# Norms stored by one transfer, the Wo product in float32r pieces, and centring moved to ACT in the last stage

## What is computed

```python
xn = _layernorm(x)
# token diffusion on layer_norm(xn) * ln1_w + ln1_b, 16 heads of 16 columns
logits = (2 * qk @ qk.T - q2[:, None] - q2[None, :]) / sqrt(dh) * tau     # q2: squared norms of qk
y = xn + (softmax(logits) @ v) @ Wo_t * gamma1
# channel diffusion on layer_norm(y) * ln2_w + ln2_b, 8 heads of 32 channels
y = y + channel_diffusion(layer_norm(y)) * gamma2
# experts on xn: relu(xn @ W1[e] + b1[e]) @ W2[e] + b2[e], times the router's gate
out = x + y + moe(xn)
```

## Time and profile before

| | |
|---|---|
| median of 3 runs | 1292.47 us (1291.58 to 1297.14) |
| the profiled execution | 1292.76 us, span 1291.0 us |
| PE busy | 1251.0 us, 97% |
| ACT busy | 1041.8 us, 81% |
| DVE busy | 439.2 us, 34% |
| POOL busy | 211.6 us, 16% |
| mean granted clock of PE | 0.995 |

### The profile page before, as it was taken

How to read it: one execution, slowest core, us unless ns; L and a number is a source line. 1 busy time by engine, 2 the same in 40 slices (tenths; PEclk the granted TensorE clock), 3 DMA queues, 4 the chain that set the end, 5 groups by cost and what they waited for, 6 DMA issues and landing times. The chain is left out here.

```text
span 1291.0 us, 42753 instructions
## 1 busy us (share of the span) xinstructions
PE 1251.0 (97%) x18451; PEld 731.6 (57%) x18451; DVE 439.2 (34%) x1226; ACT 1041.8 (81%) x1181; POOL 211.6 (16%) x310
## 2 busy tenths in 40 slices
PE   7979999999999999999999999999999999999988
PEld 6744334555555555555555555555555555555877
DVE  6732001232222223223223223222222322225957
ACT  6869999888888888888888888888888888884120
POOL 3203441111100101111111111101011111102860
PEclk9989999999999999999999999999999999999999
DMA  6798347755564564654574556456456466533573
GB/s 191 248 283 189 94 94 229 151 135 138 153 148 118 160 141 112 175 143 122 137 184 122 132 122 186 125 159 145 109 151 157 121 150 171 162 120 121 135 139 123
DMA packets 161845, 193.48 MB, mean 150 GB/s; under 512 B 64280, under 2 KB 129304, under 8 KB 158200
## 3 DMA queue, kind: packets, MB, share of 16 engines
q1 hardware_dynamic: 148392, 168.84, 49.5%
q0 software_dynamic: 13264, 21.90, 7.0%
HBM read 154.63 MB, written 35.95 MB: 148 GB/s over the span
## 5 line engine op out<-in xcount | busy, mean ns | idle before, releaser
L994 ACT ACTIVATE shared<-ps 128x1024 f32<-128x1024 f32 x1024 | 969.1, 1040 | 122.5 <-PE ps L1135 122.1
L1158 PE MATMUL ps<-shared,work 128*17 128x256 f32 x7680 | 476.6, 380 | 0.0
L1135 PE MATMUL ps<-mov,stat 52*128 52x512 f32 x2048 | 346.2, 434 | 16.0 <-ACT shared L994 9.0
L1158 PEld LDWEIGHTS ps<-shared,work 128*17 128x17 f32 x7680 | 219.5, 98 | 149.8 <-issue 24.9
L1017 DVE TENSOR_TENSOR work<-ps,work 128x256 f32<-128x256 f32 x258 | 109.5, 424 | 565.1 <-PE ps L1180 562.8
L1135 PEld LDWEIGHTS ps<-mov,stat 52*128 52x128 f32 x2048 | 167.1, 185 | 202.7 <-issue 109.3
L1171 PE MATMUL ps<-XNW,work 128*32 128x256 f32 x2496 | 196.4, 390 | 0.2 <-issue 0.2
L1180 PE MATMUL ps<-work,XNW 128*32 128x128 f32 x4992 | 191.4, 273 | 0.3 <-issue 0.3
L1180 PEld LDWEIGHTS ps<-work,XNW 128*32 128x32 f32 x4992 | 148.8, 110 | 51.6 <-issue 0.8
L842 POOL DMA_DIRECT2D y_slots<-work x39 | 22.1, 567 | 553.2 <-DVE work L1023 505.6
L1171 PEld LDWEIGHTS ps<-XNW,work 128*32 128x32 f32 x2496 | 51.8, 108 | 107.0 <-issue 100.5
(11 more groups left out here) (177 smaller groups left out, 638.6 us busy)
## 6 DMA issues: line engine op xcount, KB each, us to landing
XNW<-in_L_ffn_W_dram SPq DMA_DIRECT2D x78, 1024.0 KB, 6.1
stat<-q_parts SPq DMA_DIRECT2D x192, 128.0 KB
mov<-q_parts SPq DMA_DIRECT2D x192, 64.0 KB
q_parts<-XNW SPq DMA_DIRECT2D x16, 512.0 KB, 5.1
x_slots<-work SPq DMA_DIRECT2D x1, 4992.0 KB, 17.6
early<-x_slots SPq DMA_DIRECT2D x156, 32.0 KB, 2.2
early<-in_L_ffn_b_dram SPq DMA_DIRECT2D x39, 128.0 KB, 8.0
y_slots<-work POOLq DMA_DIRECT2D x39, 128.0 KB, 2.0
```

The costliest lines, as they stand in the source:

```text
L994: nc.scalar.activation(probs[:, q % DEEP], ps[:, at:at + 2].rearrange("p a b -> p (a b)"), ACT.Exp, scale=head_scale).then_inc(probs_ready, 1)
L1135: last = nc.tensor.matmul(ps[:, at + r], stat[rows, head % 2, m * P:(m + 1) * P], mov[rows, head % 2, half * 512:(half + 1) * 512], start= ...
L1158: last = nc.tensor.matmul(ps[32 * j:32 * j + VW, AV, half * 256:(half + 1) * 256], Vh[:, head % 2, m], probs[:, q % DEEP, j * 256:(j + 1) ...
```

## The change

- **Norms.** `w_parts` takes the whole `wp` of a group, all 128 rows, in one transfer. `fill_stack` reads the two parts by transfers of their own: 20 for a head, not 16.
- **Start.** DVE takes the statistics of group 1 ahead of z of group 0, and scales the rest of the query weights apart from that of the value weights, which now stands behind the split of group 0; PE waits for it in the first `product_v`.
- **Heads' output.** `norm_o` turns o, copies it into an upper float32r part and subtracts for the rest. Both parts are stored: 8 transfers for a head. The last head's are issued by SP, ahead of the last part of XN, not by POOL.
- **Wo.** The scaled Wo is split once into two parts. `project` runs three float32r products in place of one in float32. `AT` has four slots of one group with two parts each; the groups of batch 1 are loaded as the projection of a group four earlier is done.
- **a2.** DVE stores the negated mean (`nmr`); POOL multiplies it by the root; ACT centres and scales (`make_z2`, four activations for each group, at hand-written places in its list); DVE multiplies by `l2w` and adds `l2b`, one operation each on 1024 columns.

```diff
-    w_parts = nc.dram_tensor("w_parts", [2, NB * H, S], F32).ap()
+    w_parts = nc.dram_tensor("w_parts", [GROUPS, P, 2, GN // 2], F32).ap()
...
         def store_w(G, par):
-            b, tok = G // GB, (G % GB) * GN
             nc.sync.wait_ge(w_split, G + 1)
-            for c in range(KC):
-                for k in range(2):
-                    at = 32 * (2 * c + k)
-                    nc.sync.dma_start(w_parts[:, bass.ds(b * H + c * HC, HC), bass.ds(tok + k * GN // 2, GN // 2)]
-                                      .rearrange("c h n -> h c n"), wp[at:at + HC, par]).then_inc(w_stored[par], 16)
+            nc.sync.dma_start(w_parts[G], wp[:, par]).then_inc(w_stored[par], 16)
...
             stats_x(0, 0)
+            stats_x(1, 1)
             make_z(0, 0)
-            rest_of_weights()
+            rest_of_query_weights()
             for k in range(KC):
                 rest_of_turned(0, 0, k)
-            stats_x(1, 1)
+            rest_of_value_weights()
...
-            at_least(nc.vector, o_stored, 16 * NCHUNK * head)
-            nc.vector.transpose(o_cols, o_rows).then_inc(o_ready, 1)
+            nc.vector.transpose(o_cols, o_rows).then_inc(o_flipped, 1)
+            nc.vector.wait_ge(o_flipped, head + 1)
+            at_least(nc.vector, o_stored, O_DMAS * 16 * head)
+            nc.vector.tensor_copy(o_parts[:, 0].bitcast(F32R), o_cols).then_inc(o_upper, 1)
+            nc.vector.wait_ge(o_upper, head + 1)
+            nc.vector.tensor_tensor(o_parts[:, 1].bitcast(F32R), o_cols, o_parts[:, 0], ALU.subtract).then_inc(o_ready, 1)
...
-                sp.wait_ge(v_copied, H)
-                sp.dma_start(AT[:, 0], a_turned[0:D].rearrange("(c p) n -> p c n", p=P)).then_inc(at_loaded[0], 16)
+                sp.wait_ge(v_copied, NB * H)
+                for G in range(GB):
+                    load_at(G)
...
+                store_o(sp, HEADS - 1, last_o_stored)
                 load_xn(2)
...
+                for G in range(GB, GROUPS):
+                    sp.wait_ge(wo_ready, 2 * (G - AT_SLOTS) + 2)
+                    load_at(G)
...
-                    nc.gpsimd.tensor_tensor(rs1[:, par], ve1[:, par], nhalf[:, 0], ALU.pow).then_inc(rstd3_ready, 1)
+                    nc.gpsimd.tensor_tensor(rs1[:, par], ve1[:, par], nhalf[:, 0], ALU.pow).then_inc(rs1_step, 1)
+                    pool.wait_ge(rs1_step, G + 1)
+                    nc.gpsimd.tensor_tensor(nmr[:, par], nmr[:, par], rs1[:, par], ALU.mult).then_inc(rstd3_ready, 1)
...
+                def make_z2(G, par):
+
+                    act.wait_ge(rstd3_ready, G + 1)
+                    at_least(act, gram_done, G - 1)
+                    if G >= 2:
+                        act.wait_ge(ring3_ready, use_a2(G - 2) + KC)
+                    for t in range(GT):
+                        last = nc.scalar.activation(a2g[:, par, t], XN[:, G * GT + t], ACT.Identity,
+                                                    bias=nmr[:, par, t:t + 1], scale=rs1[:, par, t:t + 1])
+                    last.then_inc(z2_ready, 1)
...
+                make_z2(0, 0)
+                make_z2(1, 1)
                 for G in range(GB):
                     take_a2(G, G % 2)
+                    if G + 1 < GB:
+                        make_z2(G + 2, G % 2)
 
                 take_gram(0)
+                make_z2(GB + 1, 1)
                 take_t(0)
                 for tt in range(3):
                     act.wait_ge(y_stored[tt], 16 * SLOT_USES)
                 take_a2(GROUPS - 4, 0)
+                make_z2(GROUPS - 2, 0)
                 take_a2(GROUPS - 3, 1)
                 exp_of(0)
+                make_z2(GROUPS - 1, 1)
                 take_a2(GROUPS - 2, 0)
                 take_r(0)
...
                 def make_a2(G, par):
...
+                    dve.wait_ge(z2_ready, G + 1)
+                    nc.vector.tensor_tensor(a2g[:, par], a2g[:, par], l2w[:, :].unsqueeze(1).broadcast_to([P, GT, D]),
+                                            ALU.mult).then_inc(a2_step, 1)
                     dve.wait_ge(a2_step, G + 1)
...
+                    nc.vector.tensor_tensor(a2g[:, par], a2g[:, par], l2b[:, :].unsqueeze(1).broadcast_to([P, GT, D]),
+                                            ALU.add).then_inc(a2_ready, 1)
...
+                            terms = [(a, w, c) for a, w in ((0, 0), (0, 1), (1, 0)) for c in range(KC)]
+                            for n, (a, w, c) in enumerate(terms):
+                                last = nc.tensor.matmul(ps[:, 2 + k, t * D:(t + 1) * D], AT[:, slot, a, c, cols],
+                                                        wo_parts[:, w, c], start=(n == 0), stop=(n == len(terms) - 1))
```

More of the change, by code:

```diff
@@ L300, in fill_stack @@
             r0 = i * 2 * DH + hh * DH
-            w = w_parts[:, bass.ds(i * 2 + hh, 1), :].rearrange("c h n -> (c h) n")
+            head = i * 2 + hh
+            row = 2 * 32 * (head % H // HC) + head % HC
+            w = w_parts[head // H * GB:(head // H + 1) * GB, row:row + 33:32].rearrange("g k c n -> c g k n")
             for r in range(2):
@@ L310, in fill_stack @@
                                  ).then_inc(stack_loaded[hh], 16)
-                sp.dma_start(stat_raw[at + AUX + 2:at + AUX + 4, hh], w).then_inc(stack_loaded[hh], 16)
-                sp.dma_start(mov_raw[at + AUX:at + AUX + 2, hh].rearrange("d (k n) -> d k n", k=2),
-                             w.rearrange("d (k r n) -> d r k n", r=2, k=2)[:, r]).then_inc(stack_loaded[hh], 16)
+                for part in range(2):
+                    sp.dma_start(stat_raw[at + AUX + 2 + part:at + AUX + 3 + part, hh].rearrange("d (g k n) -> d g k n", g=GB, k=2),
+                                 w[part].unsqueeze(0)).then_inc(stack_loaded[hh], 16)
+                    sp.dma_start(mov_raw[at + AUX + part:at + AUX + 1 + part, hh].rearrange("d (g k n) -> d g k n", g=2, k=2),
+                                 w[part, r::2].unsqueeze(0)).then_inc(stack_loaded[hh], 16)
         def x_rows(G):
@@ L708, in product_v @@
                     nc.tensor.matmul(bank, zT[:, par, 0, c, cols], wvr[:, c], start=(c == 0), stop=False)
+                if G == 0 and t == 0:
+                    pe.wait_ge(weights_scaled, 2)
                 for c in range(KC):
@@ L783, in build @@
         o_ready = sem("o_ready")
+        o_flipped = sem("o_flipped")
+        o_upper = sem("o_upper")
+        O_DMAS = 2 * NCHUNK
         o_stored = sem("o_stored")
+        last_o_stored = sem("last_o_stored")
         ex_ready = sem("ex_ready")
@@ L828, in build, with store_o, load_at @@
         xn_back = [sem(f"xn_back{k}") for k in range(3)]
-        at_loaded = [sem("at_loaded0"), sem("at_loaded1")]
+        at_loaded = [sem(f"at_loaded{k}") for k in range(AT_SLOTS)]
         HOMES = ((0, 1, 6, 7), (2, 3), (4, 5))
-        def store_o(head):
-            nc.gpsimd.wait_ge(o_ready, head + 1)
-            rows = a_turned[head * DH:(head + 1) * DH].rearrange("d (k j n) -> j d k n", k=2, j=NCHUNK)
+        def store_o(queue, head, stored):
+            queue.wait_ge(o_ready, head + 1)
             for j in range(NCHUNK):
-                nc.gpsimd.dma_start(rows[j], o_cols[32 * j:32 * j + DH].rearrange("d (k n) -> d k n", k=2)
-                                    ).then_inc(o_stored, 16)
+                for part in range(2):
+                    rows = a_turned[part, head * DH:(head + 1) * DH].rearrange("d (k j n) -> j d k n", k=2, j=NCHUNK)
+                    queue.dma_start(rows[j], o_parts[32 * j:32 * j + DH, part].rearrange("d (k n) -> d k n", k=2)
+                                        ).then_inc(stored, 16)
+        def load_at(G):
+            b, at = G // GB, (G % GB) * GN
+            for part in range(2):
+                nc.sync.dma_start(AT_raw[:, G % AT_SLOTS, part], a_turned[part, b * D:(b + 1) * D, at:at + GN]
+                                  .rearrange("(c p) n -> p c n", p=P)).then_inc(at_loaded[G % AT_SLOTS], 16)
         def store_y(n):
@@ L960, in _ @@
                         copy_v(head + 2)
-                        store_o(head)
+                        store_o(pool, head, o_stored)
                         head += 1
@@ L1283, in build @@
         a2_ready = sem("a2_ready")
+        z2_ready = sem("z2_ready")
+        rs1_step = sem("rs1_step")
         expert_added = sem("expert_added")
@@ L1554, in project @@
                         for t in range(2):
-                            cols = slice(at + (2 * k + t) * P, at + (2 * k + t + 1) * P)
-                            for c in range(KC):
-                                last = nc.tensor.matmul(ps[:, 2 + k, t * D:(t + 1) * D], AT[:, b, c, cols], wo[:, c],
-                                                        start=(c == 0), stop=(c == KC - 1))
+                            cols = slice((2 * k + t) * P, (2 * k + t + 1) * P)
+                            terms = [(a, w, c) for a, w in ((0, 0), (0, 1), (1, 0)) for c in range(KC)]
+                            for n, (a, w, c) in enumerate(terms):
```

(2 more changed lines are left out.)

55 lines of the change are left out of this document (26 added, 29 removed).

## The result

| | before | after |
|---|---|---|
| median | 1292.65 us | 1297.42 us |
| profiled execution, span | 1292.76, 1291.0 us | 1297.0, 1295.1 us |
| first exponential | 84.06 | 83.21 |
| first projection | 1180.19 | 1178.13 |
| end of the last sum | 1288.10 | 1292.54 |

The ratio is 1.0036, 95% interval 1.0029 to 1.0043: 4.8 us slower, where 1.7 us faster was forecast, and 0.4 us above the range. By place, in the two profiled executions: the front gives 0.85 us (forecast 6.9), attention 1.2 (forecast -0.2), the last stage costs 6.5 (forecast 5.0). The front is what went wrong.

The account below looks back on a forecast made before the run. Attention's PE-ACT cycle was taken as untouched, so gains lie before it and behind, where no single engine is the limit. Front -6.9, attention +0.2, last stage +5.0 sum to -1.7 from 1292.76: 1291 us, range 1284 to 1297.

Parts of the forecast that it names:

- the front: Everything before the first exponential: start, first stall and start of attention together, -6.9 us, between -4.5 and -9.
- Start, -2.2: DVE's new order before attention: group 1's root no longer waits for DVE, ending PE's 2.37 us standstill; -2.2 us.
- First stall, -2.0: Mid-front, ACT's 4.2 us wait for a norms store: one transfer releases it 1.0 to 3.1 us sooner; -2.0 us.
- Start of attention, -2.7: SP's queue before the first exponential: first store saves 2.7, fill costs 1.2, group 5's store saves 1.2; -2.7 us.
- bound by bytes: Rival, chance 0.14: the norms' transfer lands with q and the fill is longer; front -3, time 1294.8 us.
- the fill is longer: Part of the bytes rival: filling a head's stack takes longer, helping leave the front only -3 us.
- Attention, +0.2: Head ends: DVE's extra copy and subtraction, 1.34 us together, mostly hidden; +0.2 us (0 to +1.5).
- the 1.79 of cover: At the tightest head ends, 1.79 us between DVE's last experts step and PE's weight load, hiding 1.34 us.
- Last stage, +5.0: Behind attention: POOL's product, then ACT's centring and DVE's products behind each root, delay R; +5.0 us (+3 to +6.5).
- the dear end: Last stage: upper end of the 1.8 to 3.57 us forecast for L1627's eight instructions, depending on the clock.
- Pool is not the pace: Rival, chance 0.18: PE paces the last stage, five projections save 0.56 each, -2.8; time 1283.6 us.
- POOL and DVE take turns: Rival, chance 0.10: root and product wait for DVE's 1.2 us products, +2.4 per group, +14 in all; 1305 us.

Follow-up runs that it names:

- e3: Changed kernel with DVE's order at the start as before (statistics of group 1 behind the split of group 0, all weights in one step); 1299.90 us.
- e5: Changed kernel with SP issuing each norms store first in its step, the store of group 5 ahead of the first head's stack; 1290.69 us.
- e8: Changed kernel with the edits of e5, e7 and e2 together: norms stores first, POOL's gathers thinned, a2 as before; 1286.26 us.
- e9: Changed kernel with the edits of e5 and e7 alone, a2 still centred by ACT; 1285.18 us.
- e10: e9 with x1 of group 7 ahead of the shifted logits on DVE, R's copy ahead of a2's copies on ACT; 1280.62 us, ratio to before 0.9903.
- e1: Changed kernel with the norms as before: four stores for each group, 16 transfers in a head's stack; 1295.80 us.
- e11: Changed kernel without POOL's product of negated mean and root, so the centring uses the mean unscaled; 1294.86 us.
- e2: Changed kernel with a2 made as before (no POOL product, no ACT centring, eight DVE operations per group), Wo still in pieces; 1290.92 us.
- e4: Changed kernel with heads' output and Wo product as before: one float32 part, 16 float32 instructions in a projection; 1296.58 us.
- e7: Changed kernel with POOL's gathers between the roots thinned from four each to 4, 3, 2, 2, 2, 2, 2, 2, the rest behind the last root; 1291.19 us.
- e6: Changed kernel with ACT copying turned a2 of group 6 and R ahead of centring group 7; 1296.82 us.

## Why the prediction was wrong, point by point

- **Start, -2.2.** Right, and undersized: the V copies of group 2 come 2.98 us earlier, undoing it costs 2.5 us (e3). PE's wait of 2.37 us at the earlier trace rows is gone; in its place PE waits 1.3 us, not 0.5, one group earlier.
- **First stall, -2.0. This step failed.** I let the release move by 1.0 to 3.1 us because SP issues one transfer instead of four. The stall stayed (4.2 before, 4.38 after, 3.2 to 4.1 in the five others with this front). The 3 us of issues were saved, and the landing took them back: the release came 7.8 us after the one issue (6.4 to 7.5 in the others), where it had come 7.4 us after the first of four. I had the reason in the text ("four times the bytes, behind 512 KB pieces of q") and used the landing of q at the end of the front, 5.1 us, instead of asking what it is in this stretch: 7.4 by the median. Ahead of q the store lands in 4.0 to 4.8 us (e5, e8, e9, e10), and even then nothing of that is left by group 6.
- **Start of attention, -2.7. This term was mis-sized, in sign.** It became +1.95 (the second stall grew from 6.03 to 7.98): the first exponential gained 0.85 us where the groups ahead of it had gained 2.8. The norms' reads were put at 0.24 to 0.48 each, for 1.2 us more; eight at 0.60 to 0.70, 5.1 us in all, are some 4 us more than the four of before, and the fill grew by 4.5 us (8.4 to 12.9). The row that I priced them from the earlier trace rows reads long rows in one piece; by the code the new reads collect four or eight runs of 1 KB each into one partition. The store's issue is 1.23 us, not 0.4 to 1.0, and it landed 4.9 us after it, a gain of 0.5 in place of the 1.2 taken. Undone, the norms give 1.6 us back (e1).
- **The rival "bound by bytes"** came nearest: front -3, 1294.8. Its landing is what the trace shows, and its "the fill is longer" was the larger part; it, too, was 2.6 us short.
- **Attention, +0.2.** Measured -1.2, with a copy of only 0.43 us and a subtraction of 0.69: 1.15, under the 1.79 of cover. This length lies between 1093.3 and 1097.6 us in the traces of the experiments, so no gain is claimed.
- **Last stage, +5.0.** Right in its steps. Shifted by 2.06 us, the first root was due at 1185.24 and came at 1185.09; the six periods were put at 46.2 and are 46.06; a2 of group 6 at 1237.44 and 1237.17; the variance of group 7 at 1241.94 and 1241.78; R at 1247.24 and 1246.73. The six periods match in part by luck: POOL's product makes 0.8 of the 1.7 us by which they grew (e11), not 1.8. What was under-sized is the clock: product M took 3.78 us, the dear end, so that Gram of group 7 started 5.5 us late; and it began in the same low stretch (granted 0.50 from 1246 to 1251), which cost 1.0 more. Hence +6.5, the edge of the range given. e2 puts the same 6.5 on a2 alone.
- **Pool is not the pace.** It fell: PE's period did not show, and undoing the Wo product changes nothing that can be seen (e4). A projection takes 3.10 us, not the 2.9 of the forecast, so even the price was 0.36 for each and not 0.56. e7 shows what the rival would have needed.
- **POOL and DVE take turns.** It fell as a cause: all eight roots after take 1.04 to 1.06 us. The Trainium skill's page SBUF — State Buffer, section SBUF: two separate sides, has such operations share a port. The trace of e7 agrees with it, in small: five roots there begin some 0.4 us before the end of a DVE product and take 1.31 to 1.33 us. That is some 0.3 us longer, less than the product still had to run. At 1199.49 in the kernel before a root took 1.04 us although DVE was in its scaled sum, so not every overlap costs. No run here has a root begin with a product, so a hold over its whole 1.23 us is not shown.

## What to carry to other kernels

Before a transfer is merged, ask what its landing waits for: where it lands no sooner than the bytes queued ahead of it, fewer issues give nothing, and a layout that suits one store is paid for by every read. When work is moved behind a result, the price depends on the queue that makes the result: a2 on ACT cost 6.5 us behind POOL's full list and nothing that could be seen once that list was thinned (107.1 us against 107.4, before the tail was put in order). Look at more than one trace: with the same front the same stall took 3.2 to 4.4 us. When two edits save the same time and not its sum, look for the order of small steps that both run into.

## What the runs showed of the hardware that was not expected

- A transfer that reads runs of 1 KB into one partition holds SP 0.60 to 0.70 us, one with longer runs into two partitions 0.24 to 0.44 in the same place; a store of 128 partitions (256 KB) mostly 1.23 us (0.4 to 1.5 in all), and four of 8 partitions 2.7 to 4.5 us together.
- The same 256 KB store lands 6.4 to 7.8 us after its issue behind two 512 KB pieces of q, and 4.0 to 4.8 us after it ahead of them.
- Copying 128x512 to float32r on DVE takes 0.43 us; I had priced it from a copy out of PSUM at 0.69.
- The same eight instructions of product M of batch 0 take 1.99 us in e6, where PE has waited 0.68 us for R, at a granted clock of 1.00 (the higher level, 2.4 GHz), and 3.5 to 3.8 us elsewhere at 0.50 to 0.55 (the lower, 1.2 GHz, for all or most of the time), though e2 and e10 have the same short wait: a short wait alone does not keep the higher clock, and what does is open.
